# Tops of y copied to PSUM, attention's sums inverted on ScalarE, and new orders of norm, y, fold, value weighing and first pair tiles

## The chip, the cores and the metric

The kernel runs on one core of a Trainium2 chip. The metric is the device time of one execution in microseconds. One execution in the profiler gives the trace; PE is TensorE, ACT is ScalarE, DVE is VectorE, POOL is GpSimd, SP the engine that issues DMAs.

## The reference

The input is 16 batches of 256 tokens by 128 features. Each batch goes through attention and then through an expert layer:

```
x = x + attention(layernorm(x))      # 16 heads of 8, one shared k and v, causal; y = (P v) / sum(P); y @ w_proj
xn = rmsnorm(layernorm(x), gamma)
q  = xn @ wq.T                       # 2 sides x 8 heads x 64
sim = q . keys                       # per head and side 32 scores
sx, sy = top16(sim[0]), top16(sim[1])
scores, pk = top16(all sums sx + sy) # 8 heads
h = gelu(xn . down[i]) * softmax(scores)
x = x + h @ up[i]
```

Only the first 32 x 32 = 1024 experts can be reached.

## The kernel before

Tokens lie on the 128 partitions in two tiles, j = 0 and 1. The kernel doesn't gather expert rows. For a tile and a head it forms the scores of all 1024 experts with matmuls (`pair_scores`, L1192), ScalarE turns them into probabilities (`pair_probs`, L640), and VectorE zeroes those under the 16th best (`mask`, L910). GpSimd adds the 8 heads (`add_head`, L449). The sum is transposed (`acc_transposes`, L1204), multiplied with the activations of all 1024 experts (`gate`, L931) and projected (`expert_output`, L1212).

The cut comes from VectorE: `select_keys` takes the best 16 of 32 in 16 lists per tile, and `select_pairs` adds tops of side x to tops of side y (54 candidates a head, L856, five instructions), takes the best 16, and leaves `shifted` and `cut` (L885, L889). Both inputs of the five additions lie in SBUF.

Everything is a software pipeline written by hand. The function `schedule` runs a pass `iteration(i, d, f, a, m, p)` for i = 0 to 16, passes 1 to 12 in a loop. In pass i part `f` works on the experts of batch i, part `d` finishes batch i-1, part `a` is attention of batch i+1, part `m` finds the row maxima of attention of batch i+2, and part `p` does the first norm and qkv of batch i+3. Passes 13, 14, 15 and 16 drop these parts one by one. Each engine has its own `iteration`, and the order of the calls in it is the order in which that engine works; semaphores tie the engines together. An engine that waits lets nothing behind it pass.

The steps that matter here, in the order of a pass:

- PE: `scores_for_probs` (12 steps, L1111 and L1113), with transposes of the pieces between them (L1171); `scores_for_max` (12 steps, L1081 and L1084); `weigh_values` (L1131, L1133), which multiplies the probabilities by v and by ones and so leaves y's numerator and its sums in PSUM (`misc[0]`). It waits for the copy `pieces_back` (L602) of the pass. `project_y` (L1142) needs y. `project_qkv` (L1061, L1063, L1066) needs the copy of the transposed norm (L502).
- ACT: `att_exp` (L561), `pieces_back` (L602), `max_scores_back` (12 copies, L544), `activate` (Gelu, L612, with a table load on each side, L608 and L615), `best_exp` (L621), `log_sum` (L627), then the copies of the next similarities (L589, L596) between `pair_probs`.
- DVE: `select_keys` for both tiles, `select_pairs` of tile 0, `make_y` (the reciprocal L792 and a product L794), `gate`, `make_x2` (the sum L804 and the second norm's statistics), `select_pairs` of tile 1, `sum_best`, `ln1` (the first norm's statistics, L747), `log_sum_exp`, `fold_max` (L771, L777, L784: maxima of the attention scores by halving; needs all 12 copies of L544), and then 16 masks with `qk_remainder` (L764) and `finish` (L944) between them.
- POOL: `make_xn`, `make_xhat`, `sim_low_piece`, then 14 additions `add_head` with `qk_low_piece` between them. The last additions run on into the next pass.

PSUM holds three score tiles of two banks each and two banks `misc`. The two attention banks are `score[2]`.

Of the kernel before, what the change touches and what calls it, by code (L numbers as in the profile page):

```python
# [11 lines left out]
P = 128  # L12
# [35 lines left out]
def build(nc, x, w_attn, w_proj, gamma, wq, keys, down, up, consts, out):  # L48
    ctx = ExitStack()
    with ctx:  # L50
# [157 lines left out]
        av_made = signal("av_made")  # L208
        y_inverse = signal("y_inverse")
# [22 lines left out]
        key_step = signal("key_step", TILES * KEY_STEPS)  # L232
        pair_step = signal("pair_step", TILES * PAIR_STEPS)
# [154 lines left out]
        def _(eng):  # L388
# [83 lines left out]
            def iteration(i, d, f, a, m, p):  # L472
                if a:
                    make_xn(i + 1)
                if p:
                    make_xhat(i + 3)
                if a:
                    sim_low_piece(i + 1, 0)
                    sim_low_piece(i + 1, 1)
# [17 lines left out]
        def _(eng):  # L497
# [54 lines left out]
            def att_exp(b, u):  # L552
# [8 lines left out]
                eng.activation(dst, att[u % 2][:, :], ACT.Exp, scale=float(HD) ** -0.5).then_inc(att_probs, 1)  # L561

# [80 lines left out]
            def prologue():  # L643
# [15 lines left out]
                xhat_back(2)  # L659
                for u in range(MAX_STEPS):  # L660
                    max_scores_back(1, u)
# [11 lines left out]
            def iteration(i, d, f, a, m, p):  # L673
# [10 lines left out]
                if m:  # L684
                    for u in range(6):
                        max_scores_back(i + 2, u)
                if d and f:
                    age_x2(i - 1)
                if f:
                    copy_x2(i)  # L690
                if m:
                    for u in range(6, MAX_STEPS):
                        max_scores_back(i + 2, u)
                    copy_v(i + 2)
                if f:
                    activate(i, 0)
                    activate(i, 1)
                    best_exp(i, 0)
                if a:
                    xn_back(i + 1)  # L700
                if f:
                    best_exp(i, 1)
                    log_sum(i, 0)
                    pair_probs(i, 0, 0)
                if a:
                    sim_back(i + 1, 0)
                    sim_back(i + 1, 1)
                if f:
                    pair_probs(i, 0, 1)
# [3 lines left out]
                if f:  # L713
                    pair_probs(i, 0, 2)
                if p:
                    xhat_back(i + 3)
                if f:
                    log_sum(i, 1)
                    pair_probs(i, 0, 3)
# [21 lines left out]
        def _(eng):  # L741
# [105 lines left out]
            def select_pairs(b, j):  # L847

                n = j * PAIR_STEPS
# [12 lines left out]
                n += len(PAIR_BLOCKS)  # L862
# [529 lines left out]
```

## Time and profile before

| what | value |
|---|---|
| median of 3 runs | 1073.86 us (1070.39 to 1075.57) |
| the profiled execution | 1074.99 us, span 1073.2 us |
| mean granted clock of TensorE | 0.89 of full speed |
| busiest engine | DVE, 931.1 us of 1073.2 (87%) |
| costliest group | GpSimd's additions L449, 441.7 us |

The span is the time from the first to the last instruction, and 1.8 us of the execution lie around it. Busy shares are averages over the whole span. In the chain of work that ended last, DVE has 38%, PE 34% and ACT 12%.

### The profile page before, as it was taken

The numbers are of one execution on the slowest core, as the hardware profiler recorded it, in microseconds if no ns is written. First come the engines' busy times: TensorE is split into PE (matmuls) and PEld (weight loads), VectorE is DVE, ScalarE is ACT, GpSimd is POOL, SyncE is SP. The second block draws the span as 40 slices with busy tenths as digits, with TensorE's granted clock in tenths as the row PEclk, the third lists the DMA queues.
The fourth block names the chain that finished last, engine by engine and source line by source line (L and its number), as shares of the span: only waits on it lengthen the run. The fifth ranks groups of instructions, "written<-read, shape, count | busy, mean of one in ns | idle before, by whom it ended". The sixth has DMA issues, their size and how long they took to land.

```text
span 1073.2 us, 22148 instructions
## 1 busy us (share of the span) xinstructions
PE 764.6 (71%) x6014; PEld 474.0 (44%) x6014; DVE 931.1 (87%) x4054; ACT 704.9 (66%) x1008; POOL 656.5 (61%) x371
## 2 busy tenths in 40 slices
PE   3672868686777878586777768686767878776374
PEld 2431525354444535354444535354444545353253
DVE  3327289999999999899999989899999989998987
ACT  1352677676867676676867676676867676756461
POOL 2101077694948576694948576694948576674942
PEclk9695979898998989898999989898998989797766
DMA  5312103030212103030212102030212102000000
GB/s 145 51 21 34 17 13 38 1 52 1 39 15 37 16 13 40 0 53 1 38 15 38 16 14 40 0 53 1 39 15 38 16 13 37 1 11 2 5 1 10
DMA packets 51538, 26.51 MB, mean 25 GB/s; under 512 B 5168, under 2 KB 51120, under 8 KB 51312
## 3 DMA queue, kind: packets, MB, share of 16 engines
q1 hardware_dynamic: 51504, 26.11, 15.0%
q8 instruction: 15, 0.25, 0.1%
q14 instruction: 19, 0.16, 0.1%
HBM read 19.93 MB, written 5.24 MB: 23 GB/s over the span
## 4 chain that ended last, share of the span: by engine, by line
DVE 38%; PE 34%; ACT 12%; issue 11%; DMA 1%; SPq 1%; POOL 1%; DVEq 1%; ACTq 0%; POOLq 0%
DVE prob L910 13%; DVE late_scores L777 6%; PE misc L1131 5%; ACT prob L640 4%; PE score L1192 4%; PE score L1081 4%; PE score L1111 3%; PE score L1161 3%; PE score L1204 2%; DVE cand L856 2%; PE misc L1133 2%; DVE cand_left L874 2%; ACT late_scores L544 2%; PE misc L1220 2%; DVE halves L771 2%
## 5 line engine op out<-in xcount | busy, mean ns | idle before, releaser
L449 POOL TENSOR_TENSOR acc<-acc,prob 128x1024 f32<-128x1024 f32 x186 | 441.7, 2375 | 16.6 <-DVE prob L910 0.5
L910 DVE SCALAR_TENSOR_TENSOR prob<-score,cut,prob 128x1024 f32<-128x1024 f32 x256 | 316.7, 1277 | 37.4 <-ACT prob L640 36.0
L640 ACT ACTIVATE prob<-score,neg_lse,unit 128x1024 f32<-128x1024 f32 x256 | 299.4, 1201 | 65.4 <-PE score L1192 51.3
L1192 PE MATMUL score<-sel,pieces_t 128*128 128x512 f16 x512 | 177.3, 447 | 102.3 <-DVE prob L910 97.5
L561 ACT ACTIVATE probs<-score 128x512 f32<-128x512 f32 x192 | 107.6, 599 | 64.7 <-PE score L1113 63.2
L422 POOL TENSOR_TENSOR scale<-bounded,half_neg 128x2 f32<-128x2 f32 x16 | 11.2, 703 | 202.7 <-DVE bounded L821 202.7
L1192 PEld LDWEIGHTS score<-sel,pieces_t 128*128 128x128 f16 x512 | 43.3, 108 | 183.6 <-DVE prob L910 151.6
L544 ACT ACTIVATE late_scores<-score 128x512 bf16<-128x512 f32 x128 | 69.6, 594 | 67.3 <-PE score L1084 62.2
L1111 PE MATMUL score<-q_stack,k_stack 128*128 128x512 bf16 x192 | 76.1, 401 | 45.9 <-DVE prob L910 23.5
L1081 PE MATMUL score<-k_ahead,q_ahead 128*128 128x256 bf16 (+1 forms) x512 | 75.9, 253 | 44.3 <-ACT probs L561 18.8
L449 POOL TENSOR_TENSOR acc<-prob 128x1024 f32<-128x1024 f32 x31 | 73.2, 2361 | 44.2 <-DVE prob L910 44.2
L838 DVE MATCH_REPLACE8 left<-top,sim 128x32 f32<-128x32 f32 x512 | 82.7, 173 | 0.0
L1212 PEld LDWEIGHTS misc<-wu,gated_t 128*128 128x128 f32 x512 | 70.4, 203 | 14.1 <-DVE qk_rest L764 5.8
L856 DVE TENSOR_TENSOR cand<-top 128x64 f32<-128x64 f32 (+3 forms) x160 | 76.6, 542 | 0.0
L1081 PEld LDWEIGHTS score<-k_ahead,q_ahead 128*128 128x128 bf16 x512 | 32.2, 99 | 93.4 <-ACT late_scores L544 27.8
L1212 PE MATMUL misc<-wu,gated_t 128*128 128x128 f32 x512 | 72.7, 289 | 0.0
L1220 PE MATMUL misc<-sel,ident_h 128*128 128x256 f16 x404 | 70.5, 280 | 0.0
L612 ACT ACTIVATE act_t<-score 128x1024 f32<-128x1024 f32 x32 | 32.8, 1024 | 56.9 <-PE score L1161 56.9
L1161 PE MATMUL score<-xn_t,wdt 128*128 128x128 f32 x512 | 66.8, 286 | 1.1 <-DVE gated_t L931 1.1
L1161 PEld LDWEIGHTS score<-xn_t,wdt 128*128 128x128 f32 x512 | 62.6, 200 | 2.7 <-DVE gated_t L931 1.7
L792 DVE RECIPROCAL y_t<-misc 128x256 f32<-128x256 f32 x16 | 28.0, 1750 | 38.1 <-PE misc L1133 38.1
L1113 PE MATMUL score<-cb 128*128 128x256 bf16 (+1 forms) x192 | 61.0, 318 | 0.0
(119 smaller groups left out, 1549.4 us busy)
## 6 DMA issues: line engine op xcount, KB each, us to landing
q_ahead<-q_scratch SPq DMA_DIRECT2D x96, 64.0 KB
q_stack<-q_scratch SPq DMA_DIRECT2D x96, 64.0 KB
q_scratch<-qk_piece SPq DMA_DIRECT2D x16, 192.0 KB, 2.4
xin<-x SPq DMA_DIRECT2D x16, 128.0 KB, 4.7
xres<-x SPq DMA_DIRECT2D x16, 128.0 KB, 5.1
out<-fin SPq DMA_DIRECT2D x16, 128.0 KB, 5.6
k_ahead<-qk_piece SPq DMA_DIRECT2D x96, 4.0 KB
k_stack<-qk_piece SPq DMA_DIRECT2D x96, 4.0 KB
```

What stands on the lines that cost most here:

```text
L449: eng.tensor_tensor(acc[:, j, :], so_far, prob[:, j * FH + h, :], ALU.add).then_inc(acc_added, 1)
L544: eng.activation(dst, src, ACT.Copy).then_inc(max_kept, 1)
L561: eng.activation(dst, att[u % 2][:, :], ACT.Exp, scale=float(HD) ** -0.5).then_inc(att_probs, 1)
L640: eng.activation(prob[:, g, :], score[g % BUFS][:, :], ACT.Exp, bias=neg_lse[:, j, h:h + 1], scale=unit[:, :]).then_inc(prob_made, 1)
L856: eng.tensor_tensor(dst, xs, ys, ALU.add).then_inc(pair_step, 1)
L910: eng.scalar_tensor_tensor(prob[:, g, :], score[g % BUFS][:, :], cut[:, j, h:h + 1], prob[:, g, :], ALU.is_ge, ALU.mult).then_inc(prob_mas ...
L1081: eng.matmul(bank[:, n * nk:(n + 1) * nk], q_ahead[:, h0 + n, j * P:(j + 1) * P], k_ahead[:, 0:nk], start=n == 0, stop=False)
L1111: eng.matmul(bank[:, :], k, q, start=True, stop=False)
L1161: ins = eng.matmul(score[j][:, c * P:(c + 1) * P], wdt[:, c * P:(c + 1) * P], xn_t[:, j * P:(j + 1) * P], start=True, stop=True)
L1192: ins = eng.matmul(score[g % BUFS][:, cols], pieces_t[:, j, h, :], sel[:, cols], start=True, stop=True)
L1212: ins = eng.matmul(misc[1][:, j * D:(j + 1) * D], gated_t[:, c, j * P:(j + 1) * P], wu[:, c, :], start=c == 0, stop=c == CH - 1)
L1220: eng.matmul(bank[:, 0:T], ident_h[:, :], sel[:, 0:T], start=True, stop=True)
```

## The change

- `make_y` loses its reciprocal. A new step on ScalarE, `invert_sums`, writes Ln of the sums and then Exp of minus that into `y_t`, and `make_y` only multiplies. No further table load stands in the new order of ScalarE.
- `select_pairs` is split: `sum_pairs` makes the 54 sums and `size`, `select_pairs` does the rest. For tile 0 the tops of side y are first copied to PSUM (`score[1]`), and the additions read them there. PE waits for these sums before `acc_transposes(i-1, 1)` writes `score[1]`.
- DVE: `ln1` and `make_y` move ahead of the sums of tile 0, the fold ahead of tile 1's selection, `log_sum_exp(i, 0)` in between; two masks run ahead of `sum_best(i, 1)`.
- PE: the values are weighed directly behind the attention scores, ahead of all `scores_for_max`; `project_y` stands behind four of them; `acc_transposes(i-1, 1)` behind eight; three pair tiles instead of one ahead of `key_scores`; four warming matmuls near the end of tile 0's heads.
- ACT: `max_scores_back` follows `invert_sums`, with `best_exp(i, 0)` between; `best_exp(i, 1)` and `log_sum(i, 1)` move to places between the pair tiles, and the norm's copy L502 moves one pair tile later.
- POOL: `make_xhat` ahead of `make_xn`.

```diff
+            def invert_sums(b):
+
+                eng.wait_ge(av_made, every(av_made, b))
+                if later(b):
+                    eng.wait_ge(proj_made, at(proj_made, b, 0))
+                eng.activation(y_t[:, :], misc[0][:, T:2 * T], ACT.Ln).then_inc(y_log, 1)
+                eng.wait_ge(y_log, every(y_log, b))
+                eng.activation(y_t[:, :], y_t[:, :], ACT.Exp, scale=-1.0).then_inc(y_inverse, 1)
...
             def make_y(b):
 
-                if later(b):
-                    eng.wait_ge(proj_made, at(proj_made, b, 0))
                 eng.wait_ge(av_made, every(av_made, b))
-                eng.reciprocal(y_t[:, :], misc[0][:, T:2 * T]).then_inc(y_inverse, 1)
                 eng.wait_ge(y_inverse, every(y_inverse, b))
                 eng.tensor_tensor(y_t[:, :], misc[0][:, 0:T], y_t[:, :], ALU.mult).then_inc(y_t_made, 1)
...
+            def sum_pairs(b, j):
+
                 eng.wait_ge(key_step, at(key_step, b, (j + 1) * KEY_STEPS))
+                tops_y = top[:, j, 1:LISTS:2, :]
+                if j == 0:
+                    placed = score[1][:, 0:FH * TOPK].rearrange("p (h k) -> p h k", k=TOPK)
+                    eng.tensor_copy(placed, tops_y).then_inc(top_placed, 1)
+                    eng.wait_ge(top_placed, every(top_placed, b))
+                    tops_y = placed
                 col = 0
                 for a0, na, nb in PAIR_BLOCKS:
-                    ys = top[:, j, 1:LISTS:2, 0:nb].unsqueeze(2).broadcast_to([P, FH, na, nb])
+                    ys = tops_y[:, :, 0:nb].unsqueeze(2).broadcast_to([P, FH, na, nb])
                     eng.tensor_tensor(dst, xs, ys, ALU.add).then_inc(pair_step, 1)
...
+                if p:
+                    ln1(i + 3)
+                if a:
+                    make_y(i + 1)
+                if f:
+                    sum_pairs(i, 0)
                     select_pairs(i, 0)
                 if a:
-                    make_y(i + 1)
+                    make_x2(i + 1)
                 if d:
                     gate(i - 1, 1)
-                if a:
-                    make_x2(i + 1)
-                if f:
-                    select_pairs(i, 1)
+                if f:
                     sum_best(i, 0)
-                if p:
-                    ln1(i + 3)
-                if f:
-                    log_sum_exp(i, 0)
                 if m:
                     fold_max(i + 2, 0, 6)
                 if f:
+                    sum_pairs(i, 1)
+                    log_sum_exp(i, 0)
+                    select_pairs(i, 1)
+                if f:
+                    mask(i, 0, 0)
+                    mask(i, 0, 1)
                     sum_best(i, 1)
```

DVE in the first pass before, from the end of tile 0's selection on (the rows of the loop are the same, with the gate of tile 1 between y and x2):

```order
L874 MATCH_REPLACE cand_left<-best,cand 128x54 x8
L882 MAX best<-cand_left 128x8 x8
L885 TENSOR_TENSOR shifted<-best 128x128
L889 SCALAR_TENSOR_TENSOR cut<-size,best 128x8
L792 RECIPROCAL y_t<-misc 128x256
L794 TENSOR_TENSOR y_t<-misc,y_t 128x256
L804 TENSOR_TENSOR x<-xres,misc 128x256
```

DVE in the first pass of the change, from the end of `select_keys` on:

```order
L762 BN_STATS stat<-xin 128x6 x2
L768 BN_AGGR mv<-stat 128x2 x2
L772 TENSOR_SCALAR ln_tmp<-mv 128x2
L806 TENSOR_TENSOR y_t<-misc,y_t 128x256
L865 COPY score<-top 128x128
L873 TENSOR_TENSOR cand<-top,score 128x8x16
L873 TENSOR_TENSOR cand<-top,score 128x8x8
```

The product for y now stands ahead of tile 0's sums and selection instead of behind them, the reciprocal is gone, and the norm's statistics and a copy have come in.

PE in the first pass before, from the last attention step on (L1113 ends `scores_for_probs`, L1081 and L1084 are `scores_for_max`, L1131 weighs values):

```order
L1113 MATMUL score<-cb 128x512
L1081 MATMUL score<-k_ahead,q_ahead 128x128 x4
L1084 MATMUL score<-cb 128x512
L1081 MATMUL score<-k_ahead,q_ahead 128x128 x4
L1084 MATMUL score<-cb 128x512
```

PE at the same place in the change:

```order
L1138 MATMUL score<-cb 128x512
L1156 MATMUL misc<-probs,v_blocks 32x256 x4
L1156 MATMUL misc<-probs,one_blocks 32x256 x4
L1156 MATMUL misc<-probs,v_blocks 32x256 x4
L1156 MATMUL misc<-probs,one_blocks 32x256 x4
```

The weighing has moved ahead of six `scores_for_max` steps; all twelve now come behind it.

ACT in the first pass of the change, from the last copy of the pieces (before, L602 was followed by six L544 copies, the copy of x2, and six more L544 copies):

```order
L612 ACTIVATE pieces_t<-misc 128x1024
L585 ACTIVATE x_kept<-x 128x256
L569 ACTIVATE y_t<-misc 128x256
L571 ACTIVATE y_t<-y_t 128x256
L530 ACTIVATE v_blocks<-v_next 128x8x8
L545 ACTIVATE halves<-score 128x4x128 x4
L545 ACTIVATE late_scores<-score 128x512 x5
L631 ACTIVATE exps<-shifted,unit 128x128
L545 ACTIVATE late_scores<-score 128x512 x3
L637 ACTIVATE log_total<-total 128x8
L618 ACT_TABLE_LOAD
```

The Ln and Exp of `invert_sums` (L569, L571) stand ahead of all twelve copies of maximum scores.

## Rows read from the trace of the kernel before

**Rows 1.** The page, part 1: busy us, share of the span and instructions per engine

```profile
PE 764.6 (71%) x6014; PEld 474.0 (44%) x6014; DVE 931.1 (87%) x4054; ACT 704.9 (66%) x1008; POOL 656.5 (61%) x371
```

**Rows 2.** Timeline of DVE, loop pass from 466.04 us: start, duration, line, tiles, [idle before]

```profile
466.04 1.58 DVE L832 MAX8 top<-sim 128x8 f32<-128x32 f32 x16
...
478.27 4.07 DVE L856 TENSOR_TENSOR cand<-top 128x128 f32<-128x128 f32 x5
...
486.19 1.75 DVE L792 RECIPROCAL y_t<-misc 128x256 f32<-128x256 f32 x1
...
487.98 0.42 DVE L794 TENSOR_TENSOR y_t<-misc,y_t 128x256 f32<-128x256 f32 x1
...
489.98 0.42 DVE L804 TENSOR_TENSOR x<-xres,misc 128x256 f32<-128x256 f32 x1 [0.45 <-PE misc L1142]
...
491.61 0.88 DVE L856 TENSOR_TENSOR cand<-top 128x128 f32<-128x128 f32 x5
...
496.54 0.48 DVE L747 BATCH_NORM_STATS2 stat<-xin 128x6 f32<-128x128 f32 x2
...
497.73 1.22 DVE L771 TENSOR_TENSOR halves<-late_scores 128x2048 bf16<-128x2048 bf16 x1
...
503.74 5.00 DVE L910 SCALAR_TENSOR_TENSOR prob<-score,cut,prob 128x1024 f32<-128x1024 f32 x4
...
511.88 1.28 DVE L910 SCALAR_TENSOR_TENSOR prob<-score,cut,prob 128x1024 f32<-128x1024 f32 x1 [1.81 <-ACT prob L640]
...
526.66 1.57 DVE L832 MAX8 top<-sim 128x8 f32<-128x32 f32 x16
```

**Rows 3.** Timeline of POOL in the same pass

```profile
467.30 14.64 POOL L449 TENSOR_TENSOR acc<-acc,prob 128x1024 f32<-128x1024 f32 x6
...
492.78 1.58 POOL L427 TENSOR_SCALAR xn<-x,mv,scale 128x128 f32<-128x128 f32 x2 [0.18 <-POOL scale L422]
```

**Rows 4.** Groups by line and shape, DVE, whole span: busy us, mean ns | idle before

```profile
L856 DVE TENSOR_TENSOR cand<-top 128x80 f32<-128x80 f32 x32 | 40.1, 1254 | 0.0
...
L777 DVE TENSOR_TENSOR late_scores<-late_scores 128x256 bf16<-128x256 bf16 x16 | 16.8, 1053 | 0.6
...
L777 DVE TENSOR_TENSOR late_scores<-late_scores 128x512 bf16<-128x512 bf16 x16 | 7.1, 443 | 0.5
```

**Rows 5.** Timeline of PE in the same pass

```profile
477.87 0.64 PE L1131 MATMUL misc<-probs,v_blocks 128*32 128x256 f32 x8
...
482.88 0.40 PE L1133 MATMUL misc<-probs,one_blocks 128*32 128x128 f32 x8
...
507.09 1.06 PE L1061 MATMUL misc<-xhat_t,wa 128*128 128x256 f32 x2
```

**Rows 6.** Timeline of ACT in the same pass

```profile
474.00 1.06 ACT L602 ACTIVATE pieces_t<-misc 128x1024 f16<-128x1024 f16 x1
...
483.75 3.47 ACT L544 ACTIVATE late_scores<-score 128x512 bf16<-128x512 f32 x6 [4.36 <-PE score L1084]
...
492.79 1.28 ACT L615 ACT_TABLE_LOAD   x1
...
494.09 0.40 ACT L621 ACTIVATE exps<-shifted,unit 128x128 f32<-128x128 f32 x1
...
501.15 1.16 ACT L596 ACTIVATE pieces<-sim 128x512 f16<-128x512 f32 x2
...
502.19 1.22 ACT L640 ACTIVATE prob<-score,neg_lse,unit 128x1024 f32<-128x1024 f32 x1
```

**Rows 7.** Windows: length; busy PE, PEld, DVE, ACT, POOL; granted clock; DMA share; GB/s

```profile
472.00:478.00 6.00, 4.12 (x35) 1.85 (x36) 6.00 (x63) 5.68 (x11) 5.76 (x4) 1.00 0.02 4
...
383.00:390.00 7.00, 4.94 (x17) 2.64 (x18) 6.75 (x8) 4.23 (x8) 4.74 (x3) 0.76 0.00 0
...
504.20:511.10 6.90, 5.88 (x16) 3.22 (x17) 5.80 (x6) 3.53 (x5) 4.66 (x2) 0.51 0.00 0
```

**Rows 8.** Timeline of DVE, first pass of the program

```profile
122.83 1.76 DVE L792 RECIPROCAL y_t<-misc 128x256 f32<-128x256 f32 x1 [21.17 <-PE misc L1133]
```

More of the change, by code:

```diff
@@ L477, in iteration @@
                 if a:
+                    make_xn(i + 1)
                     sim_low_piece(i + 1, 0)
@@ L659, in prologue @@
                 xhat_back(2)
+                invert_sums(0)
                 for u in range(MAX_STEPS):
@@ L683, in iteration @@
                     pieces_back(i, 1)
-                if m:
-                    for u in range(6):
-                        max_scores_back(i + 2, u)
                 if d and f:
@@ L690, in iteration @@
                     copy_x2(i)
+                if a:
+                    invert_sums(i + 1)
                 if m:
-                    for u in range(6, MAX_STEPS):
+                    copy_v(i + 2)
+                    for u in range(9):
                         max_scores_back(i + 2, u)
-                    copy_v(i + 2)
                 if f:
+                    best_exp(i, 0)
+                if m:
+                    for u in range(9, MAX_STEPS):
+                        max_scores_back(i + 2, u)
+                if f:
+                    log_sum(i, 0)
                     activate(i, 0)
                     activate(i, 1)
-                    best_exp(i, 0)
                 if a:
@@ L701, in iteration @@
                 if f:
-                    best_exp(i, 1)
-                    log_sum(i, 0)
                     pair_probs(i, 0, 0)
+                    pair_probs(i, 0, 1)
                 if a:
@@ L708, in iteration @@
                 if f:
-                    pair_probs(i, 0, 1)
+                    best_exp(i, 1)
+                if f:
+                    pair_probs(i, 0, 2)
                 if a:
@@ L713, in iteration @@
                 if f:
-                    pair_probs(i, 0, 2)
+                    log_sum(i, 1)
+                    pair_probs(i, 0, 3)
                 if p:
@@ L1010, in iteration @@
                 if f:
+                    sum_pairs(i, 1)
+                    log_sum_exp(i, 0)
+                    select_pairs(i, 1)
+                if f:
+                    mask(i, 0, 0)
+                    mask(i, 0, 1)
                     sum_best(i, 1)
-                    for h in range(4):
-                        mask(i, 0, h)
+                    mask(i, 0, 2)
+                    mask(i, 0, 3)
                     log_sum_exp(i, 1)
@@ L1283, in iteration @@
                         scores_for_probs(i + 1, u)
-                if m:
-                    for u in range(6):
-                        scores_for_max(i + 2, u)
                 if a:
@@ L1290, in iteration @@
                 if m:
-                    for u in range(6, MAX_STEPS):
+                    for u in range(4):
                         scores_for_max(i + 2, u)
+                if a:
+                    project_y(i + 1, piece_t_made, i)
+                if m:
+                    for u in range(4, 8):
+                        scores_for_max(i + 2, u)
+                if f:
+                    eng.wait_ge(pair_step, at(pair_step, i, len(PAIR_BLOCKS)))
                 if d:
                     acc_transposes(i - 1, 1)
+                if m:
+                    for u in range(8, MAX_STEPS):
+                        scores_for_max(i + 2, u)
                 if f:
                     hidden_units(i, 0)
-                if a:
-                    project_y(i + 1, piece_t_made, i)
-                if f:
                     hidden_units(i, 1)
@@ L1303, in iteration @@
                 if f:
-                    pair_scores(i, 0, 0, a, m)
+                    for h in range(3):
+                        pair_scores(i, 0, h, a, m)
                 if a:
@@ L1318, in iteration @@
                 if f:
-                    for h in range(5, FH):
-                        pair_scores(i, 0, h, a, m)
+                    pair_scores(i, 0, 5, a, m)
+                    pair_scores(i, 0, 6, a, m)
+                if p:
+                    eng.wait_ge(v_next_made, every(v_next_made, i + 3))
+                    keep_busy(misc[0], 2)
+                if f:
+                    pair_scores(i, 0, 7, a, m)
+                if p:
+                    keep_busy(misc[0], 2)
                 if m:
```

15 lines of the change are left out of this document (5 added, 10 removed).

## The prediction, made before the changed kernel ran

> **What bounds the kernel now.** I read the busy shares first: DVE works 87% of the span, no other engine over 71% [rows 1]. Then the timeline of DVE in one loop pass. A pass begins with `select_keys` at 466.04 us and the next at 526.66, so it takes 60.6 us, and the only long wait of DVE in it is 1.81 us in front of one mask [rows 2]. So work taken off DVE counts, until another engine is late. I count time from the pass's start (t = 0 at 466.04). The marks before are: sums of tile 0 at t = 12.2, y done at 22.4, fold at 31.7, masks at 37.7, the waiting mask at 45.8.
>
> Part of DVE's busy time is not work. The same five sums take 4.07 us for tile 0 and 0.88 for tile 1 [rows 2]. Of the 128x80 sum, half the instances are short, and its mean is still 1254 ns [rows 4]. The sums of tile 0 lie inside GpSimd's chain of six additions, 467.30 to 481.94 [rows 3]; those of tile 1 do not. So an operation of DVE with two SBUF inputs stands still while GpSimd adds. The masks, of which one tensor input is in PSUM, run beside such additions at 5.00 us for four [rows 2]. The fold shows it too: its 256-wide step has a mean of 1053 ns, its 512-wide one 443 [rows 4].
>
> The Trainium skill ("SBUF — State Buffer", section "SBUF: two separate sides") says why: GpSimd and DVE share a port pair under an exclusive lock, which a DVE instruction needs if it has two SBUF inputs or runs in a two-port mode, and the loser waits for the other's whole instruction. The rows agree. By that rule an addition that reads one side from PSUM needs no lock, while the norm's one-input fp32 step on SBUF, now put among GpSimd's additions, may. It would wait at most one addition, which a wait named below hides.
>
> **Part 1: the first third of a pass.** Removed from DVE: the reciprocal, 1.75 us, and the hold on tile 0's sums, 4.07 - 0.88 = 3.2 us. Added: one copy of 128x128 to PSUM. No such copy is shown; it costs more than nothing, and the product on 128x256 with a PSUM input, 0.42 us, bounds it above [rows 2]. I take 0.3. If nothing else were late, DVE would gain 4.6 us a pass here.
>
> But y is now wanted before the sums. DVE asks for it at t = 12.2 + 1.0 for the norm's statistics (496.54 to 497.73 holds them and one small step [rows 2]), so 13.3. When is it there? PE weighs the values directly behind the attention scores, but still behind the second copy of the pieces, which ends at 475.06, t = 9.0 [rows 6]. The weighing takes from 477.87 to 483.28, 5.4 us [rows 5], so it ends at 14.4. Ln and Exp on 128x256 are 0.4 us each (the Exp on 128x128 takes 0.40 [rows 6]) with 0.1 for handing over: 15.35. The product of 0.4 ends at 15.75. DVE so stands about 2.1 us in front of `make_y`, a wait that the trace before does not have. This also hides the norm's steps, held or not.
>
> Then on DVE: copy and sums 0.3 + 0.95, ending at 17.0; size and selection 3.9 (sums' end at 482.34 to the reciprocal at 486.19 [rows 2]), 20.9; x2 and statistics 1.63 (489.98 to 491.61), 22.5; gate 1.15 (between the product's end at 488.40 and x2 less its wait of 0.45), 23.7; `sum_best` 0.2, 23.9.
>
> **Part 2: the fold's inputs.** All twelve maximum copies on ACT now lie behind Ln and Exp: from 15.35 on, `v` 0.25, twelve copies at 0.58 (six take 3.47 [rows 6]), `best_exp` 0.4, and about 1.1 while PE makes room for `project_y` and the accumulator's transposes. Sum: 24.1. So the fold begins at 24.1 on two chains that arrive together: nothing is lost, but nothing is to spare. The fold took 497.73 to 503.54, 5.8 us, with holds behind the norm and pieces on GpSimd. In the new order only `xn` lies there (1.58 us [rows 3]), so I take 4.9. It ends at 29.0. Sums of tile 1, size, the small logarithm step: 1.2; selection 3.6. Masks begin at 33.8 instead of 37.7: 3.9 earlier.
>
> The table loads stay two a pass at 1.28 us, and the next activation follows at once, 494.09 behind 492.79 + 1.28 [rows 6]. The skill ("ScalarE: Activation LUTs") adds a drain of 1380 ns to each switch of set and puts exp and ln in one set. The rows show no drain; by the page's figure every switch would cost 2.66 us, in both kernels alike.
>
> ACT reaches the first pair tile in time: from 24.1, logarithm 0.2, load 1.3, two Gelus of about 1.0, load 1.3, a copy 0.4, gives 29.4, against 30.1 for the logarithm step of DVE.
>
> **Part 3: the masks.** The mask that waited in the pass before waited for a chain: `project_qkv` on PE, copy, pair scores, probability on ACT. The projection began at 507.09, t = 41.05 [rows 5], because masks 0 and 1 had to free the score tiles of the pair scores ahead of it. Now ACT sets it: `best_exp(1)` follows DVE's selection, to 34.1; a pair tile (1.22 less overlap, so 1.15) 35.2; two copies of high pieces 1.16, 36.3; the logarithm behind masks 0 and 1 and `sum_best`, 36.7; pair tile 37.8; the norm's copy 0.4, 38.2. The projection so begins at 38.25, 2.8 earlier. Behind it everything is as before, and the pass ends 2.8 us earlier, not 3.9. One more hold can lie here: `log_sum_exp(i, 1)`, two SBUF inputs, now comes just behind the start of GpSimd's second instruction of the additions and may stand up to 2.4 us, but mask 5 waits for its probability anyway, so I price it at nothing; if ACT were early it would cost those 2.4.
>
> **The sum.** Loop passes 1 to 12: 12 x 2.8 = 33.6 us. In pass 0 DVE waited 21.17 us for the weighed values [rows 8]; tile 0's selection, which lay inside that wait, now comes behind it, against an earlier weighing (it was six score steps later): 2.0. Passes 13 and 14 lack the projection or the fold, and keep the wait for y: 2.2 each. Pass 15 has no y and keeps the hold's 3.2 less the copy, of which part is lost to ACT: 2.3. Together 42. The profiled execution took 1074.99 us (span 1073.2 and 1.8 around it); less 42 is 1033. It lies 1.1 above the median of the three runs, so against that median I say 1032.
>
> **The rivals.**
> A. As summed, 1032 us. Own range 1022 to 1043.
> B. More is gained: TensorE's clock. The projection lies in stretches in which the granted clock was 0.51 in this pass and 0.76 in an earlier one [rows 7], that is partly 1.2 instead of 2.4 GHz, behind idle time of PE. The weights of time show in what a pass costs: with an earlier and denser PE and four added matmuls ahead of pair tile 7, the projection of some 1.9 us to its first result can take 1. That and an unheld fold give 0.9 more a pass, 1.3 at most: 1032 - 13 x 1.1 = 1018.
> C. Less is gained: the holds move. `shifted` of tile 0 (two SBUF inputs) now falls beside `make_xhat` on GpSimd, the fold's first step beside `xn`, and the small logarithm step beside an addition, each up to the GpSimd instruction's length, 0.8 to 2.4 us; or the twelve maximum copies come 1 to 2 us late. With 1.4 a pass lost: 1032 + 15 x 1.4 = 1053.
> D. The copy does nothing: an addition with one PSUM input is held all the same. The masks speak against it. Besides, with the wait for y the sums begin at t = 15.75, when the six additions end (481.94, t = 15.9), so only `make_xhat` could hold them, for some 1.2: 1032 + 15 x 1.2 = 1050.
> E. Slower: the weighing at 1.2 GHz. PE now idles before it, from the last attention score at about t = 6.9 to 9.0; the clock falls behind idle stretches. The 5.4 us would become 10.8, all of it on the chain to y that DVE stands before: 5.4 - 2.8 = 2.6 a pass lost, 1074 + 14 x 2.6 = 1110. It decides from a weighing of 8.2 us on. Against it: in 472 to 478, with 4.12 of 6 us busy, the granted clock was 1.00 [rows 7].
>
> **How the numbers follow.** Chances: A 0.55, B 0.17, C 0.14, D 0.05, E 0.05, and 0.04 for something that swallows all of it. Predicted is A, 1032. A, B, C and D between 1013 and 1056 hold a bit over 0.8. A difference of 0.5% (5.4 us) is about what a measurement of this kernel can tell from no change. Faster: A, B, D and nearly all of C, 0.89; within: 0.05; slower: E and a little, 0.06.
>
> **What would show it.** In the profile after: no sum of tile 0 beyond 0.35 us (D wrong), a wait of DVE of about 2 us in front of y's product, released by ACT (the chain of part 1), the weighing at 5.4 us (E wrong), the fold's first step directly behind the last maximum copy, masks starting 33.8 us into a pass, one wait for ACT of 1 to 2 us at mask 5, and a pass of 57.8 us. The prediction is wrong if the wait in front of y is much over 2 us, if two-input steps of DVE stand elsewhere, or if ACT starts the first pair tile later than DVE's logarithm step.

## The result, and the profile after

The changed kernel takes 1046.6 us (median of 4 runs, 1044.5 to 1047.5), the kernel before 1073.9 (4 runs, 1070.4 to 1075.6). The ratio is 0.9747 with a 95% interval of 0.9718 to 0.9777: faster by 27.3 us. The forecast was 1032 us, a gain of 42, with a range of 1013 to 1056. The sign, the path and the range held; a third of the gain did not come. The profiled execution has a span of 1045.6 us against 1073.2, so the traces differ by 27.6.

Part 1 of the page after, as [rows 1] (busy us, share, instructions):

```profile
PE 766.0 (73%) x6066; PEld 482.5 (46%) x6066; DVE 862.4 (82%) x4054; ACT 712.7 (68%) x1040; POOL 644.5 (62%) x371
```

DVE is busy 68.7 us less, more than twice what the time fell: about 28 of it is the 16 reciprocals, most of the rest are holds that are gone. Part of what was given back is idle time in front of y.

The timeline of DVE after, of the loop pass that begins at 454.75 us (the answer to [rows 2]; the columns are the same):

```profile
454.75 1.57 DVE L844 MAX8 top<-sim 128x8 f32<-128x32 f32 x16
...
470.26 0.42 DVE L806 TENSOR_TENSOR y_t<-misc,y_t 128x256 f32<-128x256 f32 x1 [2.06 <-ACT y_t L571]
470.60 0.28 DVE L865 COPY score<-top 128x128 f32<-128x128 f32 x1
470.92 0.86 DVE L873 TENSOR_TENSOR cand<-top,score 128x128 f32<-128x128 f32 x5
...
478.70 1.33 DVE L786 TENSOR_TENSOR halves<-late_scores 128x2048 bf16<-128x2048 bf16 x1
...
483.31 0.87 DVE L873 TENSOR_TENSOR cand<-top 128x128 f32<-128x128 f32 x5
...
488.09 2.47 DVE L930 SCALAR_TENSOR_TENSOR prob<-score,cut,prob 128x1024 f32<-128x1024 f32 x2
...
493.38 1.44 DVE L921 SCALAR_TENSOR_TENSOR neg_lse<-best,neg_unit,log_total 128x8 f32<-128x8 f32 x1
...
497.43 1.28 DVE L930 SCALAR_TENSOR_TENSOR prob<-score,cut,prob 128x1024 f32<-128x1024 f32 x1 [1.41 <-ACT prob L650]
```

Read it beside the forecast. The wait in front of y is 2.06 (about 2.1), the copy 0.28 (0.3), the sums of tile 0 cost 0.86 like those of tile 1 (0.95), the fold begins 24.0 into the pass (24.1), the masks at 33.3 (33.8), and one wait for ACT stands at mask 5 (1.41). The next pass begins at 512.2, after 57.5 us (57.8 forecast).

ACT and PE before that wait for y:

```profile
469.32 0.38 ACT L569 ACTIVATE y_t<-misc 128x256 f32<-128x256 f32 x1 [4.76 <-PE misc L1158]
469.74 0.42 ACT L571 ACTIVATE y_t<-y_t 128x256 f32<-128x256 f32 x1
```

```profile
463.86 0.64 PE L1156 MATMUL misc<-probs,v_blocks 128*32 128x256 f32 x8 [2.24 <-issue]
...
468.84 0.43 PE L1158 MATMUL misc<-probs,one_blocks 128*32 128x128 f32 x8
```

The weighing takes 5.4 us from 9.1 into the pass; ACT idles 4.76 us before Ln, Ln and Exp take 0.8, then DVE gets y. PE stands 2.24 us before the weighing. That gap decides much of what follows. The profile puts it down to "issue", since PE's sequencer was in the wait for the second copy of the pieces.

Then I read all sixteen passes, each from its first `select_keys` instruction to the next one's, and pass 15 to the end of the program (us, worked out from the timeline of DVE):

```
pass      0     1     2     3     4     5     6     7     8     9     10    11    12    13    14    15
before  79.05 59.80 60.53 60.63 59.72 60.55 60.62 59.73 60.55 60.63 59.73 60.55 60.63 56.68 57.52 70.52
after   77.99 59.39 57.48 57.47 59.02 57.47 57.47 59.08 57.47 57.47 59.11 57.48 57.47 57.57 57.34 70.41
gain     1.06  0.41  3.05  3.16  0.70  3.08  3.15  0.65  3.08  3.16  0.62  3.07  3.16 -0.89  0.18  0.11
```

Eight passes gain 3.1, more than the forecast 2.8. Passes 1, 4, 7, 10 gain 0.4 to 0.7, and 13 to 15 nothing. Passes 1, 4, 7 and 10 stand out in both rows: before they were the short ones, after they are the long ones. In pass 7 the weighing, which starts as far into the pass as ever, takes 7.0 us:

```profile
521.33 1.08 PE L1156 MATMUL misc<-probs,v_blocks 128*32 128x256 f32 x8 [2.24 <-issue]
...
523.86 1.00 PE L1156 MATMUL misc<-probs,one_blocks 128*32 128x256 f32 x8
524.67 0.62 PE L1156 MATMUL misc<-probs,v_blocks 128*32 128x256 f32 x8
```

Two windows over the two weighings (columns as in [rows 7]; the granted clock is the third number from the end):

```profile
463.50:469.30 5.80, 5.44 (x130) 4.33 (x131) 4.56 (x46) 0.97 (x3) 5.64 (x3) 1.00 0.28 43
521.00:528.40 7.40, 7.08 (x131) 4.66 (x132) 4.50 (x46) 0.94 (x3) 7.24 (x4) 0.77 0.36 47
```

The first four groups of matmuls take 1.0 to 1.1 us each instead of 0.64, and the window's granted clock is 0.77: a stretch at 1.2 GHz and the rest at 2.4. These four groups last 3.3 us instead of 1.7, which costs 1.6 us of the pass. I call it a dip.

Last, passes 13 to 15. A small step on DVE, [idle before] none:

```profile
900.36 1.50 DVE L921 SCALAR_TENSOR_TENSOR neg_lse<-best,neg_unit,log_total 128x8 f32<-128x8 f32 x1
...
956.80 1.74 DVE L921 SCALAR_TENSOR_TENSOR neg_lse<-best,neg_unit,log_total 128x8 f32<-128x8 f32 x1
...
1006.76 2.19 DVE L921 SCALAR_TENSOR_TENSOR neg_lse<-best,neg_unit,log_total 128x8 f32<-128x8 f32 x1
```

Eight elements a partition, and up to 2.19 us where others of its kind take 0.21: it has two SBUF inputs and stands behind an addition of GpSimd. It ends when that addition ends: in the pass shown above the step runs from 493.38 to 494.82, and GpSimd beside it from 492.45 to 494.80:

```profile
492.45 2.35 POOL L451 TENSOR_TENSOR acc<-prob 128x1024 f32<-128x1024 f32 x1
```

### The profile page after: what moved, and what is told of

Read it like the earlier page. It is cut to its first block, busy times and chain, and to the rows that moved or that the text cites. A ratio compares the mean times of both kernels' runs of the same rounds, so it can differ in the third digit from the quotient of the medians.

```text
span 1045.6 us, 22349 instructions
## 1 busy us (share of the span) xinstructions
PE 766.0 (73%) x6066; PEld 482.5 (46%) x6066; DVE 862.4 (82%) x4054; ACT 712.7 (68%) x1040; POOL 644.5 (62%) x371
## 4 chain that ended last, share of the span: by engine, by line
DVE 38%; PE 34%; issue 16%; ACT 8%; DMA 1%; SPq 1%; POOL 1%; DVEq 1%; ACTq 0%; POOLq 0%
DVE prob L930 13%; PE misc L1156 7%; PE score L1136 5%; PE score L1217 4%; ACT prob L650 4%; DVE late_scores L792 4%; DVE cand_left L894 4%; PE misc L1158 3%; PE score L1138 3%; DVE best L888 3%; DVE best L902 2%; DVE cand L873 2%; PE misc L1245 2%; DVE halves L786 2%; PE score L1229 2%
## 5 line engine op out<-in xcount | busy, mean ns | idle before, releaser
L438 POOL TENSOR_TENSOR pieces<-sim,pieces 128x512 f16<-128x512 f32 x32 | 36.4, 1159 | 145.1 <-ACT pieces L606 145.1
L1245 PE MATMUL misc<-sel,ident_h 128*128 128x256 f16 x456 | 82.1, 283 | 0.0
L1156 PE MATMUL misc<-probs,v_blocks 128*32 128x256 f32 x512 | 46.5, 428 | 34.4 <-issue 34.4
L806 DVE TENSOR_TENSOR y_t<-misc,y_t 128x256 f32<-128x256 f32 x16 | 6.8, 425 | 78.5 <-ACT y_t L571 78.5
L569 ACT ACTIVATE y_t<-misc 128x256 f32<-128x256 f32 x16 | 6.1, 384 | 87.2 <-PE misc L1158 87.2
L1186 PE MATMUL score<-xn_t,wdt 128*128 128x128 f32 x512 | 62.2, 281 | 3.8 <-DVE gated_t L951 3.8
L1245 PEld LDWEIGHTS misc<-sel,ident_h 128*128 128x128 f16 x456 | 46.9, 103 | 38.8 <-issue 10.5
```

Of the source, the lines that this page charges most:

```text
L1156: eng.matmul(rows, block, probs0[:, 4 * g + m, :], start=m + n == 0, stop=False)
L1245: eng.matmul(bank[:, 0:T], ident_h[:, :], sel[:, 0:T], start=True, stop=True)
```

## Experiments

Every ratio is against the kernel before on the same chip, with its 95% interval. "Dips" are counted in the profiled execution. A pass means an undipped one of passes 2 to 12. The experiments ran on different chips, on which the kernel before took 1073.9 to 1076.0 us, so a difference between two medians is good to about 2 us; the ratios don't have that error.

**1. Is the gap before the weighing needed?** `weigh_values` waits until both transposed copies of the pieces are out of `misc`; it writes only where the first has been read.

```
 # weigh_values, PE (after)
-                    eng.wait_ge(reader, every(reader, of_batch))
+                    eng.wait_ge(reader, at(reader, of_batch, 1))
```

> The changed kernel, but the weighing of values waits only for the first of the two copies of the pieces (the one that reads its bank), not for both. Theory: the wait for y that DVE shows (2.06 us a pass) and the granted clock's fall inside the weighing, which in the profile after hit passes 1, 4, 7, 10, 13 and 14 and cost 1.6 us in each, both come from the 2.24 us in which PE stands before the weighing. It should then start 2.0 us earlier, y start at 13.5 us into a pass instead of 15.5, no pass show y at 17, and passes take about 55.5 us: some 1012 to 1018 us in all. Rival: the clock dips have nothing to do with that idle time, or the fold's maxima on ScalarE arrive late instead; then passes take 57 us and more and the time stays above 1030.

Measured: 1015.7 us, ratio 0.9451 (0.9431 to 0.9471), 31 us below the changed kernel. That is as expected (1012 to 1018). A pass takes 55.57. The weighing starts at 7.2 instead of 9.1, and DVE hardly waits:

```profile
454.56 0.42 DVE L806 TENSOR_TENSOR y_t<-misc,y_t 128x256 f32<-128x256 f32 x1 [0.19 <-ACT y_t L571]
```

```profile
448.16 0.64 PE L1156 MATMUL misc<-probs,v_blocks 128*32 128x256 f32 x8 [0.34 <-issue]
```

So the whole chain from that gap to y did set the pass, microsecond for microsecond: 1.9 earlier at the weighing, 1.9 off the pass. Dips remain in passes 3, 5, 10 and 14, now in the attention scores at the pass's start, behind the idle time of PE at the end of the pass before:

```profile
382.73 0.59 PE L1136 MATMUL score<-q_stack,k_stack 128*128 128x512 bf16 x1 [1.67 <-DVE prob L930]
...
385.45 0.64 PE L1245 MATMUL misc<-sel,ident_h 128*128 128x256 f16 x2
...
386.37 0.38 PE L1245 MATMUL misc<-sel,ident_h 128*128 128x256 f16 x2
```

**2. Fill the gap instead.** The wait stays where it is; 14 matmuls that nobody reads run in it.

```
 # tensor engine, iteration (after)
                 if a:
+                    eng.wait_ge(piece_t_made, at(piece_t_made, i, 1))
+                    keep_busy(misc[0], 14)
                     weigh_values(i + 1, 0, piece_t_made, i)
```

> The changed kernel with 14 extra matmuls of 256 columns into the free bank in front of the weighing, behind the first copy of the pieces; the start of the weighing isn't moved. It isolates the clock. Theory (the dip costs 1.6 us in 6 of 14 passes because PE idles before it): every pass has y at 15.5 us and takes 57.5, in all 8 to 10 us less than the changed kernel: 1037 to 1039. Rival (the dip follows from the stretch as a whole, or the matmuls delay the weighing): no gain, 1045 to 1050.

Measured: 1041.9 us, 0.9690 (0.9672 to 0.9707), 4.8 below the changed kernel. In the trace every weighing of passes 1 to 12 takes 5.4 us, so the dip behind the gap is gone. But in passes 7, 10 and 13 the weighing starts at 10.7 instead of 9.1: the dip lies ahead of it, and costs the same 1.57. In pass 7 it lies in the attention scores and ends near 509 us, where the same matmul falls from 0.63 to 0.38:

```profile
508.48 0.63 PE L1136 MATMUL score<-q_stack,k_stack 128*128 128x512 bf16 x1
...
509.28 0.38 PE L1136 MATMUL score<-q_stack,k_stack 128*128 128x512 bf16 x1
```

The gain is about half of what I had put down. With the gap filled there are three dips where the changed kernel had seven (passes 0, 1, 4, 7, 10, 13 and 14), and they lie elsewhere in the pass.

**3. Leave out the copy.** The sums read `top` on both sides.

```
 # sum_pairs, DVE (after)
-                if j == 0:
+                if False:
                     placed = ...
```

> The changed kernel without the copy to PSUM: tile 0's sums read both sides from SBUF again. Theory (prediction, rival D's arithmetic): the sums begin when the six additions of GpSimd end, since DVE waits for y first, so the hold is at most that of the two norm instructions (0.61 us each in the profile after) plus what is left of an addition; the copy saves 0.3 itself. Result within 0.3 to 1.0 us a pass of the changed kernel: 1046 to 1058. Rival (the copy is what the gain rests on): the old hold of 3.2 us a pass comes back, about 1090.

Measured: 1046.1 us, 0.9736 (0.9720 to 0.9753): no difference from the changed kernel, at the lower edge of what was expected (1046 to 1058). Its undipped passes take 57.47 to 57.52, the same within 0.05. The sums are held a little, by as much as the copy costs:

```profile
466.60 0.42 DVE L806 TENSOR_TENSOR y_t<-misc,y_t 128x256 f32<-128x256 f32 x1 [2.09 <-ACT y_t L571]
466.95 1.30 DVE L873 TENSOR_TENSOR cand<-top 128x128 f32<-128x128 f32 x5
```

1.30 against 0.28 + 0.86 and a gap. And the fold waits for the last maximum copy of ACT anyway. Since y now comes first, the six additions are over when the sums begin; the order did the copy's work. Only pass 15, which has no y to wait for, gets the old hold back, and there the pass is 0.5 us longer (70.96 instead of 70.41):

```profile
984.18 3.94 DVE L873 TENSOR_TENSOR cand<-top 128x128 f32<-128x128 f32 x5
```

**4. The copy alone, in the old order.** To `before` I added the copy and the one wait on PE that it needs, so that the accumulator's transposes stay off the borrowed score tile.

```
 # select_pairs, DVE (before)
+                tops_y = top[:, j, 1:LISTS:2, :]
+                if j == 0:
+                    placed = score[1][:, 0:FH * TOPK].rearrange(...)
+                    eng.tensor_copy(placed, tops_y).then_inc(top_placed, 1)
+                    ...
 # tensor engine, ahead of acc_transposes(i - 1, 1)
+                if f:
+                    eng.wait_ge(pair_step, at(pair_step, i, len(PAIR_BLOCKS)))
```

> The kernel before, with only the copy to PSUM for tile 0's sums (and PE's wait for them before it writes that score tile). Theory: the hold of 3.2 us a pass goes, the copy costs 0.3, and the reciprocal and all orders stay; y's inputs are there (the weighing ends 1 us before DVE now wants them at 14.3+3.9 us into the pass), so DVE gains 2.9 us a pass in 14 of them, 1074 - 40 = 1034, which would be as good as the whole change. Rival: what DVE gains is lost by waiting for the weighed values, the projection of y or the maxima, and the kernel gains 1 us a pass or less, 1060 or above.

Measured: 1066.1 us, 0.9925 (0.9906 to 0.9945). I had expected 1034; the rival came instead. First what the copy does, where GpSimd really adds. POOL, then DVE:

```profile
464.85 14.56 POOL L450 TENSOR_TENSOR acc<-acc,prob 128x1024 f32<-128x1024 f32 x6
```

```profile
475.83 0.27 DVE L855 COPY score<-top 128x128 f32<-128x128 f32 x1
476.14 0.86 DVE L863 TENSOR_TENSOR cand<-top,score 128x128 f32<-128x128 f32 x5
```

Both stand in the middle of the chain of additions (464.85 to 479.41), and the sums take 0.86 instead of 4.07 [rows 2]. With one side in PSUM the hold is gone. This is the rule of the Trainium skill ("SBUF — State Buffer", section "SBUF: two separate sides"), that a DVE operation needs the lock that it shares with GpSimd when both inputs are in SBUF; this trace agrees. The copy itself, with one SBUF input, is not held either. y so comes 2.84 us earlier. But the fold begins at 31.82, no earlier than before [rows 2], and passes take 58.8 to 60.8. What DVE gained it stands again in front of the gate and x2, for PE in its old order (pass 2; the waits of pass 6 are the same):

```profile
245.38 1.22 DVE L938 TENSOR_TENSOR gated_t<-score,act_t 128x1024 f32<-128x1024 f32 x1 [2.04 <-PE score L1211]
247.77 0.42 DVE L805 TENSOR_TENSOR x<-xres,misc 128x256 f32<-128x256 f32 x1 [1.17 <-PE misc L1149]
```

**5 to 7. The parts and the orders apart.** Number 5 gives the changed kernel the reciprocal on DVE again; 6 does so and leaves out the copy, so only the new orders stay; 7 puts both parts into the old orders, Ln and Exp ahead of the six late maximum copies.

```
 # 5 and 6: invert_sums on ACT is empty; make_y, DVE (after)
                 eng.wait_ge(av_made, every(av_made, b))
+                eng.reciprocal(y_t[:, :], misc[0][:, T:2 * T]).then_inc(y_inverse, 1)
                 eng.wait_ge(y_inverse, every(y_inverse, b))
 # 7: before, with the copy of number 4, and on ACT behind copy_x2(i)
+                if a:
+                    invert_sums(i + 1)
```

> The changed kernel with y's sums inverted by VectorE's reciprocal again (1.75 us), no Ln and Exp on ScalarE; all orders and the copy kept. Theory: VectorE stands in front of y anyway, so the move to ScalarE is worth not 1.75 us a pass but the difference of the two ways from the end of the weighing to y: 1.75 against Ln and Exp with their hand-over, 0.9. y's product at 16.3 us into a pass instead of 15.5, 0.8 us in 15 passes, 1056 to 1060 us. Rival: the reciprocal's full 1.75 us is lost: 1070 or more; or ScalarE, freed 0.8 us earlier for the maxima, makes up for it: 1046.

> Only the new orders on all engines: neither the copy to PSUM nor Ln and Exp. Theory: the holds are avoided by the order (the sums begin when GpSimd's additions end), and y is early because of PE's order, so most of the gain stays: as with the reciprocal alone put back, 1056 to 1060 us, that is 15 to 18 us under the kernel before. Rival: without its two new parts the change is worth little, 1070 and more.

> Both new parts in the old orders: the kernel before with the copy to PSUM and with Ln and Exp on ScalarE directly ahead of the six late copies of maxima. VectorE has 4.6 us less to do in a pass. Theory: in the old order of PE, y's projection stands behind the accumulator's transposes and the first hidden units, so x2 waits for PE (as with the copy alone, where the sums came 3.2 us earlier and the fold began no earlier): the gain over the copy alone is under 3 us in all, 1062 to 1067. Rival: each part gives its own time, 1074 - 15 x 4.3 = 1010.

Measured:

```
orders  copy  Ln/Exp  kernel             us      ratio (95%)                pass
old     -     -       before           1074.6 to 1076.0                    60.5 to 60.6; 59.7 in four
old     yes   -       copy_only        1066.1  0.9925 (0.9906 to 0.9945)   58.8 to 60.8
old     yes   yes     parts_old_order  1082.8  1.0055 (1.0034 to 1.0077)   61.4
new     -     -       order_only       1057.2  0.9825 (0.9800 to 0.9851)   58.7
new     yes   -       recip_back       1054.4  0.9802 (0.9786 to 0.9818)   58.25
new     -     yes     no_copy          1046.1  0.9736 (0.9720 to 0.9753)   57.5
new     yes   yes     changed kernel   1046.6  0.9747 (0.9718 to 0.9777)   57.5
```

By the ratios the orders alone gain some 19 us. On top of them Ln and Exp gain 10, or 6 where the copy is there; the copy gains 2 or 3, and nothing once Ln and Exp are there. Number 6 lies in its expected range; number 5 lies 2 us under its own (1056 to 1060), with one dip in passes 1 to 12 instead of four. In number 5, with the reciprocal, DVE waits 1.12 for PE, works 1.76 on it and makes y 0.86 later, and the pass is 0.78 longer:

```profile
468.83 1.76 DVE L802 RECIPROCAL y_t<-misc 128x256 f32<-128x256 f32 x1 [1.12 <-PE misc L1156]
470.62 0.42 DVE L804 TENSOR_TENSOR y_t<-misc,y_t 128x256 f32<-128x256 f32 x1
```

Number 7 went the wrong way for all that I had put down (1062 to 1067): DVE has over 4 us less to do in each pass, and the kernel is slower than before. DVE and PE in it:

```profile
492.35 0.42 DVE L805 TENSOR_TENSOR y_t<-misc,y_t 128x256 f32<-128x256 f32 x1 [2.18 <-ACT y_t L572]
495.99 1.23 DVE L948 TENSOR_TENSOR gated_t<-score,act_t 128x1024 f32<-128x1024 f32 x1 [3.21 <-PE score L1221]
498.38 0.42 DVE L815 TENSOR_TENSOR x<-xres,misc 128x256 f32<-128x256 f32 x1 [1.17 <-PE misc L1159]
```

```profile
483.42 0.63 PE L1101 MATMUL score<-cb 128*128 128x512 bf16 x1
...
485.50 1.07 PE L1148 MATMUL misc<-probs,v_blocks 128*32 128x256 f32 x8
486.35 0.65 PE L1148 MATMUL misc<-probs,one_blocks 128*32 128x256 f32 x8
```

DVE stands 6.6 us, at three places. ACT, held in Ln for the weighing, copies the late maxima later; PE waits for ACT, and the accumulator's transposes, on which the gate hangs, come behind. The weighing also begins at 1.2 GHz in every loop pass; the clock has fallen already in the maximum scores ahead of it. Against number 4 it begins 0.8 us later and ends 1.3 us later (18.5 instead of 17.2 into the pass), and the fold begins 1.5 later. So the slow clock alone could make up most of the loss against number 4; how much each of these costs was not measured apart.

**8 and 9. The projection earlier.** In the changed kernel the norm's copy on ACT (`xhat_back`) waits behind pair tile 3, and PE projects behind it. Number 8 moves the copy one tile ahead, on top of number 1; number 9 does so alone.

```
 # scalar engine, iteration
-                    pair_probs(i, 0, 3)
                 if p:
                     xhat_back(i + 3)
                 if f:
+                    pair_probs(i, 0, 3)
                     pair_probs(i, 0, 4)
```

> The kernel with the early weighing, and ScalarE's copy of the transposed norm one pair tile earlier, where it stood before the change. Theory: mask 5 waits 1.4 us a pass for a chain that starts with the projection of qkv, and the projection waits for this copy (0.83 us on PE), so it should start about 0.8 to 1.1 us earlier and passes take 54.6 us instead of 55.6, 1001 to 1006 us in all. Rival: the projection then waits for the pair tiles ahead of it on PE (masks 0 and 1), or the small logarithm step held behind GpSimd (1.44 us) now stands on the path: no gain, 1013 to 1017.

> The changed kernel with one of its moves undone: ScalarE copies the transposed norm ahead of pair tile 3 again, not behind it. Theory: the projection of qkv, which mask 5 waits for, starts about 1 us earlier, and in the early-weighing kernel the same move made passes 0.9 us shorter; so 57.5 becomes 56.6 in the 12 full passes, 1034 to 1038 us. Rival: that gain was bound to the early weighing; 1043 or more.

Measured: number 8 takes 996.0 us, 0.9260 (0.9244 to 0.9275), 19.7 below number 1, where I had thought of 10 to 14 (1001 to 1006 us). A pass takes 54.67, 0.9 less, and none of passes 3 to 12 has a dip. Number 9 takes 1038.9, 0.9666 (0.9647 to 0.9685), 7.8 below the changed kernel and just above what I expected (1034 to 1038). Its undipped passes take 55.98, 1.5 less, but 10 of the 12 now have a dip and take 57.5 to 57.9. The same move gains 20 in one setting and 8 in the other. In passes 1 to 12 of the traces the dips make the difference: three were there and went in number 8; four were there in the changed kernel and ten are in number 9. Its trace is of an execution that took 1033.1 us: of six, two took 1033, at a granted clock of 0.901 and 0.904, and four 1038.6 to 1040.2, at 0.896 to 0.898. So dips can differ between executions of one kernel.

**10 and 11. The held small step.** `log_sum_exp(i, 1)` goes one mask ahead, to where less of an addition is left to run; alone, and on top of number 8.

```
 # vector engine, iteration
+                    log_sum_exp(i, 1)
                     mask(i, 0, 3)
-                    log_sum_exp(i, 1)
```

> The changed kernel with the small logarithm step of tile 1 one mask earlier, ahead of mask 3. In the profile after it stands 1.44 us (its work is 0.2) behind a GpSimd addition. Theory: in the 12 full passes mask 5 waits for ScalarE anyway and the hold is free there, as the prediction priced it; in passes 13, 14 and 15, where no mask waits for the projection, it is on the path, and those three holds (1.3 to 2.2 us each) are what is to be had: 3 to 5 us in all, ratio to the changed kernel 0.995 to 0.997. Rival 1: the hold is on the path in every pass: 15 us and more. Rival 2: the step is held just as long by the GpSimd instruction before: nothing.

> The fastest kernel so far (early weighing, norm's copy ahead of pair tile 3) with the logarithm step one mask earlier. In it the step stands 1.20 us and mask 5 still waits 0.28 us for ScalarE. Theory: full passes stay within 0.1 us of 54.7, passes 13 to 15 gain 1 to 2 us each: 991 to 994 us. Rival: the hold's end and mask 5's wait are so near to each other that full passes gain too, 985 or less; or none gain, 996.

Measured: number 10 takes 1041.5 us, 0.9689 (0.9670 to 0.9707), 5 below the changed kernel, where 3 to 5 were expected. The pass times that follow are of its profiled execution, which took 1037.5. Its undipped full passes take 57.47 to 57.49, unchanged, so in them the hold is free: it ends ahead of the wait at mask 5, which grows from 1.41 to 2.52. Pass 13 takes 54.26 instead of 57.57, and 14 takes 53.65 instead of 57.34. Of that, 1.6 and 1.7 were there by mask 0 (the dips that this run has not) and 1.7 and 2.0 came behind it: the hold. Pass 15 stays long, at 70.66 (70.41 in the changed kernel). From its first mask on it is 2.2 us shorter, though the step is still held for 1.16 there, but the first mask comes 2.5 us later. The additions of the pass before now end 17.6 us into the pass instead of 15.6, and PE's transposes, with DVE's gate behind them, wait for that:

```profile
967.86 14.79 POOL L451 TENSOR_TENSOR acc<-acc,prob 128x1024 f32<-128x1024 f32 x6
```

```profile
982.79 1.94 PE L1229 MATMUL score<-ident,acc 128*128 128x128 f32 x8 [13.60 <-POOL acc L451]
```

With DVE quicker, GpSimd is what is late in that pass. Number 11 takes 992.5 us, 0.9238 (0.9221 to 0.9255), as expected (991 to 994), and is the fastest kernel of this study, 54 us below the changed one; its granted clock is 0.903 over the span (0.887 in the changed kernel), and the wait for y is gone in passes 1 to 12:

```profile
444.42 0.83 DVE L772 TENSOR_SCALAR ln_tmp<-mv 128x2 f32<-128x2 f32 x1
445.16 0.41 DVE L806 TENSOR_TENSOR y_t<-misc,y_t 128x256 f32<-128x256 f32 x1
```

## Why the prediction was right, and by how much it was off

**Right: the path.** The chain from the pieces' second copy over the weighing, Ln and Exp to y bounds the first third of a pass, and the last maximum copy the fold; experiment 1 showed the first of these by moving it, and every mark of an undipped pass was met within 0.6 us. **Right: what limits the gain is no longer DVE.** Also right, and only argued then: the additions with one side in PSUM run free (experiment 4). But by the prediction's own signs of being wrong one came: a two-input step of DVE does stand elsewhere, `log_sum_exp(i, 1)` with 1.44 us in every pass. It was named and priced at nothing, which held in passes 1 to 12 alone.

**Off: the sum, by 15 us**, in these terms of it:

- *"Loop passes 1 to 12: 12 x 2.8 = 33.6"* measured 27.3. The traced pass of before took 60.62, but four of the twelve take only 59.7, and the mean is 60.31, which takes 3.8 off. I had read one pass where the trace held twelve. [rows 7] could have told: in the projection's window the granted clock was 0.76 in pass 4, one of the short ones, and 0.51 in pass 6, and mask 5 waits 0.89 in the one and 1.81 in the other. A clock with a period of three passes was there before the change. The new undipped pass is 57.47 and not 57.8, which gives 4.2 back. The dips in passes 1, 4, 7 and 10 take 6.7.
- *The dips are rival E in small.* I gave it 0.05 and priced it as all or nothing: the whole weighing at 1.2 GHz in all passes, 1110 us. It came in one pass of three, for the first four groups of matmuls, 1.7 of the 5.4 us, at a price of 1.6. The window that spoke against it [rows 7] showed one pass, and that was one without a dip. A price per pass and a share of passes should have stood there.
- *"Passes 13 and 14 ... 2.2 each. Pass 15 ... 2.3"* measured -0.6 together, 7.3 less. I had seen the hold of `log_sum_exp(i, 1)` and priced it at nothing, since mask 5 waits for its probability anyway. That is so in passes 1 to 12 (experiment 10: unchanged). In 13 to 15 there is no projection for mask 5 to wait for, the cover is gone, and the hold is paid: some 1.7 and 2.0 in 13 and 14. The same two passes have a dip each. In pass 15 the first mask waits 2.34 for ACT, which I had put into the term only in words. Up to that mask the pass is 1.9 us ahead of the kernel before (26.3 against 28.2 into the pass), 0.4 less than forecast; from there to the end it loses 1.8, and the step held for 2.19 instead of 0.21 lies there. So most of the missing 2.2 was lost behind the first mask, where the hold lies.
- *Pass 0: 2.0* measured 1.06; its weighing has a dip too (7.1 us).

The terms add up: 6.3 + 7.3 + 0.9 = 14.5 of 42 less, that is 27.5, against 27.6 in the spans.

**The other rivals.** D (the addition is held all the same) is false, by experiment 4. But its second half was true and should have become a forecast: with y first, "only `make_xhat` could hold them". That says that the copy is worth next to nothing here, and experiment 3 found that. The 3.2 us of hold that I listed as removed by the copy were removed by the order, in all passes but 15. C named three holds; `shifted` did not come (0.29 as before), the fold's first step hardly (1.33 against 1.22), and the third, the small logarithm step, did. B's denser clock did not come in the changed kernel: the projection begins at 37.7, close to the 38.25 forecast, but the clock over the span is 0.887 against 0.890.

**Missed altogether:** the wait for the second copy of the pieces. I used its end (t = 9.0) as the time from which PE may weigh, and did not ask whether the weighing needs it. It doesn't, and leaving it out was worth 31 us, more than the change itself.

## What to carry to other kernels

A stage's new order can do the work of a new operation: price the operation in the order in which it will stand, not in the one where the hold was seen. When a wait is said to hide a cost, list the passes that don't have the wait; the first and last passes of a software pipeline usually lack something. And read the length of every pass ahead of the sum: one typical pass hides a clock that falls in one pass of three.

## What the runs showed of the hardware

- **The lock takes no account of size.** A step on 128x8 with two SBUF inputs took 1.44 to 2.19 us beside GpSimd's 2.36 us additions, and 0.21 where none ran. The masks, with one tensor input in PSUM, ran at 1.28 us beside the same additions. The Trainium skill ("SBUF — State Buffer", section "SBUF: two separate sides") says that the loser waits for the whole instruction; the rows agree.
- **One SBUF input is not always free.** The norm's step on 128x2 fp32, one SBUF input, took 0.37 us in the changed kernel's pass shown and 0.83 in that of experiment 11 (2.07 in its pass 1), where it fell among the additions, against 0.17 where none ran. I had allowed for up to one addition, and that is what came. What sets the size is how much of the addition is left: the step of experiment 11, 444.42 to 445.25, ends 0.03 us behind the addition that it fell into, and so do all the others that were held in these two traces (0.02 to 0.03):

```profile
442.87 2.35 POOL L451 TENSOR_TENSOR acc<-acc,prob 128x1024 f32<-128x1024 f32 x1
```

- **GpSimd gains as well.** Its `xhat` instructions took 1.06 and 1.41 us in the kernel before, beside DVE's fold with two SBUF inputs, and take 0.62 and 0.61 us where DVE now has sums that read PSUM (first before, then after). `xn` went the other way, from 1.58 [rows 3] to 2.19, since it now lies beside the fold:

```profile
498.36 1.06 POOL L397 TENSOR_TENSOR xhat<-xin,mv 128x256 f32<-128x256 f32 x1
499.56 1.41 POOL L401 TENSOR_TENSOR xhat<-xhat,rstd 128x256 f32<-128x256 f32 x1
```

```profile
471.23 0.62 POOL L399 TENSOR_TENSOR xhat<-xin,mv 128x256 f32<-128x256 f32 x1
471.99 0.61 POOL L403 TENSOR_TENSOR xhat<-xhat,rstd 128x256 f32<-128x256 f32 x1
```

- **The granted clock falls in some passes of equal work.** Which ones differed from kernel to kernel, and in number 9 from one execution to another: every third pass in the changed kernel (behind its 2.24 us gap), 3, 5, 10 and 14 in experiment 1, every pass in 7, 10 of 12 in 9, none of 3 to 12 in 8. A dip cost 1.0 to 1.7 us of its pass (a few tenths of the weighing and 0.8 us ahead of it in 7). Why a gap brings a dip in one pass and not in the next was not settled; I found nothing in the passes' rows that tells them apart.
